# Last layer's attention of a four-layer model: the value projection moved to the head of a step, and the reciprocals moved behind the maxima

## The reference

```python
def _L3_attn_ref(x, Wq, Wk, Wv, Wo, bo, rel_pos_bias):
    B, T, _ = x.shape
    H, dh = (N_HEADS, D_HEAD)
    q = (x @ Wq).reshape(B, T, H, dh).transpose(0, 2, 1, 3)
    k = (x @ Wk).reshape(B, T, H, dh).transpose(0, 2, 1, 3)
    v = (x @ Wv).reshape(B, T, H, dh).transpose(0, 2, 1, 3)
    logits = jnp.einsum('bhqd,bhkd->bhqk', q, k)
    causal = jnp.where(j > i, -jnp.inf, 0.0)
    logits = logits + causal[None, None] + _pos_bias(rel_pos_bias, T)[None]
    logits = logits / dh
    probs = jax.nn.softmax(logits, axis=-1)
    out = jnp.einsum('bhqk,bhkd->bhqd', probs, v)
    out = out.transpose(0, 2, 1, 3).reshape(B, T, H * dh)
    return out @ Wo + bo
```

## Time and profile before

| | us |
|---|---|
| median of 3 runs | 3793.6 |
| lowest and highest | 3791.26, 3796.87 |
| the profiled execution | 3826.92 |
| its span, first to last instruction | 3825.1 |
| this attention, all of its stage | about 2960 to 3743 of the span |

### The profile page before, as it was taken

How to read it: one execution, slowest core, us unless ns; L and a number is a source line. 1 busy time by engine, 2 the same in 40 slices (tenths; PEclk the granted TensorE clock), 3 DMA queues, 4 the chain that set the end, 5 groups by cost and what they waited for, 6 DMA issues and landing times. The chain is left out here.

```text
span 3825.1 us, 87256 instructions
## 1 busy us (share of the span) xinstructions
PE 3345.6 (87%) x26852; PEld 2091.7 (55%) x26852; DVE 2373.0 (62%) x6059; ACT 2026.3 (53%) x4169; POOL 1563.8 (41%) x2652
## 2 busy tenths in 40 slices
PE   4799999999967999859999867979874999999997
PEld 2344444777632222237777523679762666666664
DVE  5688887323346888667777755178356565666564
ACT  5588888443354888813333343333344666666662
POOL 0266667000011233227777626055571444444440
PEclk9799999999966999979999878878696999999999
DMA  5423322000022121145665211300033333333330
GB/s 135 105 70 76 74 72 63 22 6 12 4 74 63 48 47 44 26 93 156 162 159 158 77 64 37 104 6 3 13 59 73 102 117 117 117 117 117 117 97 23
DMA packets 200113, 289.70 MB, mean 76 GB/s; under 512 B 41100, under 2 KB 157004, under 8 KB 199520
## 3 DMA queue, kind: packets, MB, share of 16 engines
q1 hardware_dynamic: 195748, 277.81, 26.7%
q0 software_dynamic: 4096, 8.40, 1.4%
HBM read 234.81 MB, written 35.93 MB: 71 GB/s over the span
## 5 line engine op out<-in xcount | busy, mean ns | idle before, releaser
L779 ACT ACTIVATE att_E<-att_pX,att_gs 128x512 f32<-128x512 f32 x1152 | 718.0, 683 | 133.0 <-PE att_pX L708 132.3
L1957 POOL TENSOR_TENSOR att_E<-att_E,att_rz 128x128 f32<-128x128 f32 (+3 forms) x512 | 357.4, 719 | 436.1 <-DVE att_rz L2167 436.1
L834 DVE TENSOR_REDUCE att_mx<-att_pS 128x2 f32<-128x1024 f32 (+2 forms) x448 | 434.7, 992 | 86.7 <-PE att_pS L686 71.9
L686 PE MATMUL att_pS<-arr_ks,arr_qs 72*128 72x512 bf16 (+4 forms) x1536 | 423.0, 339 | 50.7 <-DVE att_mx L834 27.6
L708 PE MATMUL att_pX<-arr_qs,arr_ks 75*128 75x512 bf16 (+4 forms) x1536 | 420.8, 329 | 8.9 <-DMA arr_qs<-att_mp 4.8
L1697 POOL TENSOR_TENSOR pairs_h<-pairs_m,pairs_r 128x512 f32<-128x512 f32 x272 | 345.6, 1271 | 194.0 <-DVE pairs_m L1760 129.1
L1721 PEld LDWEIGHTS pairs_po<-pairs_a,pairs_h 128*128 128x128 f32 x2176 | 286.5, 192 | 130.4 <-issue 129.2
L826 DVE CUSTOM_DVE_ANT_0 att_seen<-att_pS,arr_later 128x384 bf16<-128x384 f32 (+1 forms) x512 | 298.8, 613 | 80.4 <-PE att_pS L686 80.0
L1742 ACT ACTIVATE pairs_r<-pairs_ph 128x512 f32<-128x512 f32 x272 | 162.4, 597 | 330.1 <-PE pairs_ph L1713 328.9
L721 PE MATMUL att_pO<-att_E,att_vs 128*9 128x512 f32 (+3 forms) x3072 | 298.5, 491 | 9.2 <-ACT att_E L779 8.7
L2099 ACT ACTIVATE att_E<-att_S,att_nm 128x128 f32<-128x128 f32 (+3 forms) x512 | 283.0, 557 | 40.3 <-DVE att_nm L2161 40.1
(11 more groups left out here) (413 smaller groups left out, 6458.9 us busy)
## 6 DMA issues: line engine op xcount, KB each, us to landing
pairs_c<-weights SPq DMA_DIRECT2D x272, 256.0 KB, 3.9
att_bias<-in_bias_dram SPq DMA_DIRECT2D x64, 896.0 KB, 5.1
parts<-proj_part SPq DMA_DIRECT2D x144, 128.0 KB, 2.3
att_xb<-xnT SPq DMA_DIRECT2D x64, 256.0 KB, 5.4
arr_qs<-parts SPq DMA_DIRECT2D x192, 64.0 KB
arr_ks<-parts SPq DMA_DIRECT2D x192, 64.0 KB
att_w<-in_w3a_dram SPq DMA_DIRECT2D x64, 192.0 KB, 5.1
arr_qs<-parts SPq DMA_DIRECT2D x96, 96.0 KB
```

What stands on the lines that cost most here:

```text
L686: ins = nc.tensor.matmul(pS[:, bank, n * w:(n + 1) * w], qs[:K1, u, x, q * P:(q + 1) * P], ks[:K1, u, x, :w], start=(n == 0 or not causal) ...
L779: nc.scalar.activation(E[:, c % NE], pX[:, BANK2[(g * NP2 + c) % (NB * NP2)]], ACT.Exp, scale=gs[:, g % 2, gain_of:gain_of + 1]).then_inc( ...
L834: V.reduce_max(dst, src, AX.X).then_inc(s_mx, 1)
L1957: nc.gpsimd.tensor_tensor(E[:, k, :width(j)], E[:, k, :width(j)], rz[:, u, k:k + 1].broadcast_to([P, width(j)]), ALU.mult).then_inc(s_n, 1)
```

## The change

The value projection of the next pair becomes the first work of step j = 0 on TensorE, ahead of the weighing and the scores. ScalarE's copy of it goes ahead of the copy of the outputs. The values get four places (VR) in the place of two, and the copy waits for a pair four before to be weighed. On VectorE the reciprocals of each step go behind the maxima of that step. Nothing is computed otherwise than before.

```diff
@@ layer3_attention
-    RING, WR = 4, 8
+    RING, WR, VR = 4, 8, 4
...
-        v = p.sb("v", [P, 2, QT, P])
+        v = p.sb("v", [P, VR, QT, P])
@@ TensorE, weigh
-                            ins = nc.tensor.matmul(pO[cols, j * P:(j + 1) * P], v[:, u, k, cols], WT[:, (2 * t_ + h) % WR, k * P:(k + 1) * P],
+                            ins = nc.tensor.matmul(pO[cols, j * P:(j + 1) * P], v[:, t_ // QT % VR, k, cols], WT[:, (2 * t_ + h) % WR, k * P:(k + 1) * P],
@@ TensorE, body
                     for s in range(STEPS):
                         m, j = divmod(s, QT)
+                        if j == 0 and not (last and m + 1 >= PAIRS):
+                            project(at, 2, m + 1, first)
                         if j % 2 == 0:
                             for t_ in (s - 2, s - 1):
                                 if not (first and t_ < 0):
                                     weigh(at, t_, first)
                             for t_ in (s + AHEAD, s + AHEAD + 1):
                                 if not (last and t_ >= STEPS):
                                     scores(at, t_, first)
-                        if j == 0 and not (last and m + 1 >= PAIRS):
-                            project(at, 2, m + 1, first)
@@ ScalarE, leave
-                    if not (first and m < 2):
-
-                        if k < 2:
-                            act.wait_ge(s_sc, at(STEPS, QT * (m - 1)))
-                        else:
-                            act.wait_ge(s_o, at(STEPS, QT * (m - 1)))
-                    dst = (qT[:, u], kT[:, u], v[:, u].rearrange("p q f -> p (q f)"))[k]
+                    if k < 2 and not (first and m < 2):
+                        act.wait_ge(s_sc, at(STEPS, QT * (m - 1)))
+                    if k == 2 and not (first and m < VR):
+                        act.wait_ge(s_o, at(STEPS, QT * (m - VR + 1)))
+                    dst = (qT[:, u], kT[:, u], v[:, m % VR].rearrange("p q f -> p (q f)"))[k]
@@ ScalarE, body
+                        if j == 0 and not (last and m + 1 >= PAIRS):
+                            leave(at, 2, m + 1, first)
                         if j == 0 and not (first and m == 0):
                             outputs(at, m - 1, first and m == 1)
-                        if j == 0 and not (last and m + 1 >= PAIRS):
-                            leave(at, 2, m + 1, first)
@@ VectorE, body
-                        if not (last and s + 2 >= STEPS):
-                            invert(at, s + 2, first)
                         if not (last and s + AHEAD >= STEPS):
                             extreme(at, 2 * (s + AHEAD), first)
                             extreme(at, 2 * (s + AHEAD) + 1, first)
+                        if not (last and s + 2 >= STEPS):
+                            invert(at, s + 2, first)
```

## The result

The changed kernel takes **3881.9 us** (median of 4 runs, 3877.4 to 3883.1) against 3792.4 for the kernel before (4 runs): a ratio of 1.0232, with a 95% interval from 1.0214 to 1.0249. It is slower by 89.5 us; forecast were 3879 and +85. The profiled execution has a span of 3879.2 us. In the stage itself nothing of that is left: from its first query projection to the next stage's first matmul it takes 3796.7 - 2918.9 = 877.8 us, and took 3744.3 - 2952.7 = 791.6. That is **+86.2 us**.

The account below looks back on a forecast made before the run. TensorE was taken to bound the kernel, in flight 675 of 700 us. A pair of 2.87 + 1.68 + 4.92 + 3.92 = 13.39 against 12.06 gave +85 on the median 3793.6: 3879 us, range 3845 to 3898.

Parts of the forecast that it names:

- key projection to value projection: TensorE's stretch up to the moved projection, which must wait for ScalarE's copy of the keys; forecast 1.81 us.
- scores to short weighing: TensorE's third stretch of a pair, forecast 4.92 us against 4.93 before; by TensorE alone it would be 3.37.
- fifth and sixth row turned at: When GpSimd's two divided rows of step 2 are ready for TensorE's transposes: 3.66 and 4.44 us after the scores' start.
- pair: One period of TensorE's work over two heads, the sum of its stretches: 13.39 us forecast against 12.06, +1.33.
- The removed wait: TensorE's output projection no longer waits for ScalarE's copy of the values: 0.50 us a pair gone.
- The chain behind the swap: Scores, maxima, late reciprocals, GpSimd's products, sixth row: 4.44 us, hidden with the swap alone, uncovered by moving the projection.
- The new wait for the keys' copy: The value projection starts 0.07 or 0.14 us after ScalarE's copy of the keys; 1.81 instead of 1.43.
- The clock: TensorE's clock stays at 1.00, costing nothing; rival: it falls around the turns, 3900 to 4007 us, chance 0.04.
- Rival 1: The reciprocals' delay is covered and the removed wait shows: pair 11.84, -0.22, time 3780 us; chance 0.06.
- The sum: Whole-kernel total: 83.8 us for 63 pairs plus 1.7 for the last pair, together +85 us.
- The last pair: The pair without a value projection: its scores to short weighing goes from 3.19 to 4.92 us, +1.7.
- The offset between profiled and unprofiled execution: The profiled execution before was 33 us above the median of the runs; no row showed where those lie.

Follow-up runs that it names:

- swap_only: The kernel before with the reciprocals moved behind the maxima and nothing else; 3795.3 us, ratio 1.0006.
- swap_later_still: From swap_only, the reciprocals of a pair's step 2 also put behind the 128x128 maxima; 3820.4 us, ratio 1.0071.
- v_between_swap: From swap_only, the value projection moved between the weighing and the scores, two places of values; 3863.7 us, ratio 1.0177.
- v_first_only: The changed kernel with the reciprocals left ahead of the maxima, so only projection and value places change; 3786.6 us, ratio 0.9977.
- v_between: The kernel before with the value projection between the weighing and the scores, reciprocals still ahead of the maxima; 3773.4 us, ratio 0.9938.
- behind_not_j0: The changed kernel with the reciprocals ahead of the maxima in step j = 0, behind them in the other three; 3782.8 us, ratio 0.9968.
- behind_at_j0: The changed kernel with the reciprocals behind the maxima in step j = 0 alone, ahead in the other three; 3878.6 us, ratio 1.0218.
- v_between_act7: From v_between, the copy of a pair's last turned row (512 wide) given from VectorE to ScalarE; 3748.6 us, ratio 0.9880.

## Why the prediction was right

Term by term, start to start, out of the timeline of the changed kernel:

| stretch | before | forecast | after |
|---|---|---|---|
| key projection to value projection | | 1.81 | 1.79 |
| value projection to weighing | | 1.06 | 1.09 |
| the two together, with no projection before | 1.53 | 2.87 | 2.88 |
| weighing to scores | 1.68 | 1.68 | 1.68 |
| scores to short weighing | 4.93 | 4.92 | 4.92 |
| of it, fifth and sixth row turned at | | 3.66, 4.44 | 3.66, 4.45 |
| short weighing to key projection | 3.92 | 3.92 | 3.92 |
| pair | 12.06 | 13.39 | 13.40 |

- *The removed wait.* It is gone as said, 0.50 us a pair. It bought nothing by itself in the changed kernel, since the stretch in which it lay is as long as before.
- *The chain behind the swap* was the deciding step. Its length, from durations of operations that had never stood in this order, is right to 0.01. That it costs only together with the moved projection was written down as well, with 0.07 us of cover; swap_only (no change) and swap_later_still (+0.41 a pair for 0.42 more of delay) show both.
- *The new wait for the keys' copy* came out at the shorter of the two latencies that the rows gave, and 0.02 under it: 1.79 for 1.81, so 0.36 us of wait. v_between_swap shows that it is real.
- *The clock* stayed at 1.00 through the 700 us, with gaps of about 1.0 and 0.5 us before the turned rows. The reason given for this was weak: the window of the next stage had fewer matmuls, but TensorE was busy for all of its 56 us, so it says nothing of gaps. And at the head of the stage the clock does fall once more than before, which was forecast only as a rival (last section); it costs some 1.7 us. By the Trainium skill (TensorE: Matmul & The Clock Gate, Part 4) the transpose mode doesn't count as TensorE being busy in the way other matmuls do. No cost of that is seen in the 700 us; but only 20 of the 96 matmuls of a pair are transposes, so this doesn't refute the rule.
- *Rival 1*, the faster end, turned on the sixth row being free at 2.94; that is true in v_first_only, and there the sign is the rival's. What it gains is less than written (7 to 9 us, not 13): 0.17 a pair instead of 0.22, and five pairs that are 0.34 longer, with the same 0.35 lost by VectorE as in v_between, and gone in behind_not_j0.
- *The sum.* 63 x 1.33 + 1.7 = 85 against 86.2 in the stage and 89.5 in the runs (81 to 94 by the interval of the ratio). The 83.8 for the 63 pairs is the substance of it. That the rest fits to 1 us is luck, since two errors cancel. The last pair was put at +1.7, and its scores to short weighing do go from 3.19 to 4.92 (3783.44 to 3788.36). But before, TensorE waited behind that short weighing for VectorE's copy, and this wait is gone:

```profile
3736.70 1.43 PE L2008 MATMUL att_pT<-ident,att_E 128*128 128x128 f32 x8 [1.11 <-DVE att_WT L2175]
```

```profile
3789.17 1.37 PE L2008 MATMUL att_pT<-ident,att_E 128*128 128x128 f32 x8
```

From its weighing to the next stage's first matmul the last pair takes 14.99 (from 3781.76), after 14.51 (from 3729.84): +0.5 and not +1.7. Against it stand the 1.7 us of the clock. The offset between profiled and unprofiled execution, which I had left open, was no part of this stage.

## What to carry to other kernels

Moving work out of a stretch also takes away cover: ask which chain of other engines ends in that stretch, and how long it is from the same start. Here two edits that cost nothing or gain a little alone lost 2.3% together. In a pipeline written by hand, an order of two pieces need not be the same in every step; it was wrong in one step of four and free in the other three. The place that gained is between the weighing and the scores: the keys' copy is done while TensorE weighs (3304.06, and the value projection starts at 3305.53 in v_between), and the values' copy while it makes the scores (3307.33, and the output projection starts at 3308.39), so neither wait arises.

## What the runs showed that was not expected

In the profile of before, an earlier stage, the output of the third layer's attention (its projection is L2911 before and L2909 after) ran from 2853.9 to 2909.9, 56 us, and in the profile of after from 2839.3 to 2875.9, 37 us:

```profile
L2911 PE MATMUL out_py<-out_wos,out_gt x128: 273/275/581, 2853.9 to 2909.9; 128*128 128x128 f32 x128
```

```profile
L2909 PE MATMUL out_py<-out_wos,out_gt x128: 273/275/579, 2839.3 to 2875.9; 128*128 128x128 f32 x128
```

The windows of that stretch have the same work (160 matmuls), and the share of time in which the DMA engines were busy is 0.65 in 71 us and 0.86 in 52. The nine other kernels profiled here leave that stage as it is, and in all of them the last layer's attention begins between 2915.8 and 2923.4, as in the profile of after (2918.9), and not where it begins in that of before (2952.7). So some 19 of the 33 us by which the profiled execution of before stood above its median are one slow stage of one execution; the rest had been lost before it, since the stage begins at 2853.9 there and at 2839.3 in the profile of after. Why it was slow there no run shows. Spans of two single executions may differ by such a thing: a stage is better compared from its own first to its own last instruction.

At the head of the last attention, before its steady part, the changed kernel has its new wait for GpSimd too, and right behind it the granted clock falls to its lower level for 3.4 us. In the profile of before it is 1.00 at that place, 25 us into the stage:

```profile
2943.14 0.55 PE L2008 MATMUL att_pT<-ident,att_E 128*128 128x128 f32 x3 [1.45 <-POOL att_E L1957]
...
2944.30:2947.70 3.40, 3.40 (x22) 2.22 (x20) 1.13 (x5) 0.02 (x1) 1.57 (x2) 0.54 0.87 331
```

```profile
2974.90:3000.00 25.10, 23.60 (x193) 16.30 (x192) 13.77 (x53) 16.01 (x48) 11.13 (x16) 1.00 0.35 111
```

Both kernels have one such fall about 7 us earlier (granted 0.51 before and 0.55 after). Of the eleven kernels profiled, the three in which TensorE waits for the late reciprocals with the projection moved (the changed kernel, behind_at_j0 and v_between_swap) show the second fall, and no other does. So the wait is the likely cause; no experiment tested it. What ran at half the clock for 3.4 us would have taken 1.7 us less.

Right behind the stage the clock falls once more, after TensorE has stood for 2.38 us:

```profile
3797.30:3800.70 3.40, 3.40 (x6) 1.37 (x5) 0.59 (x1) 0.60 (x1) 0.00 (x0) 0.59 0.00 0
```

Nine of the eleven profiles have this, and in them the next stage takes 61.0 to 61.4 us from its first L1818 to its last. The profile of before (with the same 2.38 us of standing) and that of v_between_act7 do not show it, and there it takes 59.7. So it doesn't go with the change, but a comparison with this one profile of before makes a kernel look up to 1.7 us slower than it is.
